# Causal mask of the softmax attention: added by VectorE in PSUM instead of by two TensorE products

## What is computed

```python
xn = x / jnp.maximum(l2, 1e-12) * scale_norm * gamma
qkv = jnp.einsum('bnc,fc->bnf', xn, w_qkv)          # 16 sequences, n = 256, 8 heads of 128
q = q * scale_attn
sim = jnp.einsum('bihd,bjhd->bhij', q, k)           # 256 x 256 per sequence and head
sim = jnp.where(causal_mask, neg, sim)              # j > i is masked
attn = jax.nn.softmax(sim, axis=-1)
out = jnp.einsum('bhij,bjhd->bihd', attn, v)
return jnp.einsum('bnf,cf->bnc', out.reshape(b, n, DIM_INNER), w_out)
```

## Time and profile before

| | |
|---|---|
| median of 3 runs | 3316.56 us (3315.86 to 3318.93) |
| the profiled execution | 3332.27 us, of it the profiled span 3330.6 us |
| mean granted TensorE clock | 0.879 of full speed |
| attention stage, first to last row maximum (127 units apart) | 1030.7 to 1386.0 us |
| busy in the span | PE 2336.7 us (70%), DVE 2420.9 (73%), ACT 1562.2 (47%), POOL 1600.5 (48%) |

### The profile page before, as it was taken

How to read it: one execution, slowest core, us unless ns; L and a number is a source line. 1 busy time by engine, 2 the same in 40 slices (tenths; PEclk the granted TensorE clock), 3 DMA queues, 4 the chain that set the end, 5 groups by cost and what they waited for, 6 DMA issues and landing times. The chain is left out here.

```text
span 3330.6 us, 60036 instructions
## 1 busy us (share of the span) xinstructions
PE 2336.7 (70%) x16660; PEld 1743.5 (52%) x16660; DVE 2420.9 (73%) x5876; ACT 1562.2 (47%) x3151; POOL 1600.5 (48%) x1352
## 2 busy tenths in 40 slices
PE   6636666754928999758343777678888847788887
PEld 2212222233827888648232555466767624676766
DVE  3479999963546666534446777489999966999998
ACT  2355455521714555326222444356666623566665
POOL 0176666614030000040324444289999901999996
PEclk9869899985968999959676999789999965999999
DMA  1000000012010000111100000100000000000000
GB/s 45 0 0 0 0 0 0 0 51 84 24 44 20 0 0 0 52 32 41 41 13 1 2 0 0 29 1 0 0 0 0 0 3 0 1 0 0 0 0 26
DMA packets 61385, 42.72 MB, mean 13 GB/s; under 512 B 7795, under 2 KB 55940, under 8 KB 61190
## 3 DMA queue, kind: packets, MB, share of 16 engines
q1 hardware_dynamic: 56070, 32.09, 3.4%
q0 software_dynamic: 4096, 8.40, 0.8%
q10 hardware_dynamic: 1120, 1.06, 0.1%
HBM read 27.38 MB, written 14.16 MB: 12 GB/s over the span
## 5 line engine op out<-in xcount | busy, mean ns | idle before, releaser
L1601 POOL TENSOR_TENSOR k7a_psums<-k7a_sims 128x1024 f32<-128x1024 f32 x224 | 422.8, 1912 | 189.4 <-ACT k7a_sims L1707 159.0
L1601 POOL TENSOR_TENSOR k5a_psums<-k5a_sims 128x1024 f32<-128x1024 f32 x224 | 422.7, 1913 | 77.3 <-ACT k5a_sims L1707 48.1
L725 POOL TENSOR_TENSOR mc_hc<-mc_h,mc_cs 128x512 f32<-128x512 f32 x256 | 324.8, 1269 | 149.7 <-DVE mc_h L708 149.1
L1661 PE MATMUL k7a_pw<-g_ident,k7a_w 128*128 128x128 f32 x2048 | 272.7, 279 | 87.7 <-DVE k7a_hid L1793 47.9
L1661 PE MATMUL k5a_pw<-g_ident,k5a_w 128*128 128x128 f32 x2048 | 272.2, 279 | 84.8 <-DVE k5a_hid L1793 47.9
L708 DVE TENSOR_TENSOR_SCAN mc_h<-mc_dA,mc_dbu 128x512 f32<-128x512 f32 x256 | 310.0, 1211 | 0.0
L1661 PEld LDWEIGHTS k7a_pw<-g_ident,k7a_w 128*128 128x128 f32 x2048 | 223.5, 141 | 147.9 <-DVE k7a_w L1784 92.2
L1661 PEld LDWEIGHTS k5a_pw<-g_ident,k5a_w 128*128 128x128 f32 x2048 | 223.2, 141 | 145.2 <-DVE k5a_w L1784 89.6
L637 PE MATMUL mc_y<-mc_hc,g_ident 128*128 128x512 f32 x512 | 257.7, 626 | 45.0 <-DVE m_sz L694 43.0
L667 ACT ACTIVATE mc_dA<-m_delta,m_A 128x510 f32 (+1 forms) x256 | 176.6, 690 | 227.3 <-DVE mc_h L708 227.2
L1784 DVE SCALAR_TENSOR_TENSOR k5a_w<-k5a_psums,k5a_best,k5a_lift 128x1024 f32<-128x1024 f32 x224 | 279.0, 1269 | 0.5 <-ACT k5a_lift L1722 0.3
(11 more groups left out here) (589 smaller groups left out, 5936.7 us busy)
## 6 DMA issues: line engine op xcount, KB each, us to landing
e_ZS<-sorted_rows SPq DMA_DIRECT2D x8, 640.0 KB, 7.4
sorted_out<-e_YS SPq DMA_DIRECT2D x8, 640.0 KB, 3.6
e1p_w<-in_L_ffn_W_dram SPq DMA_DIRECT2D x16, 256.0 KB, 5.5
e3p_w<-in_L_ffn_W_dram SPq DMA_DIRECT2D x16, 256.0 KB, 5.4
sorted_rows<-e_ZS SPq DMA_DIRECT2D x1, 2560.0 KB, 10.9
g_X<-in_L_attn_a_x_dram SPq DMA_DIRECT2D x8, 256.0 KB, 6.0
out_dram<-g_X SPq DMA_DIRECT2D x1, 2048.0 KB, 8.7
sorted_rows<-e_YS,e_slot POOLq DMA_INDIRECT x64
```

What stands on the lines that cost most here:

```text
L725: nc.gpsimd.tensor_tensor(hc[:, q % RH, :], h_[:, q % RB, :], cs[:, s % 2, :], ALU.mult).then_inc(outs, 1)
L1601: nc.gpsimd.tensor_tensor(psums[:, h - 1, :, :], rows_of(p, h), s2, ALU.add).then_inc(pooled, 1)
L1661: ins = nc.tensor.matmul(pw[:, j, :], w[:, h % WR, j * P:(j + 1) * P], env.ident[:, :], start=(h == 0 and j % 4 == 0), stop=(h == HD - 1 a ...
```

## The change

VectorE adds the mask. TensorE no longer computes the two bf16 products, and its two score products now start their blocks themselves. In `maxima`, a `tensor_tensor` adds `env.causal` (bf16, the same table for both blocks) to columns 0 to 127 and 256 to 383 of the score bank, read from and written to PSUM. Its own new semaphore `masked` is waited for by the first reduction.

```diff
@@ score (TensorE)
-                    nc.tensor.matmul(S[:, 0:P], env.identb[:, :], env.causal[:, :], start=True, stop=False)
-                    nc.tensor.matmul(S[:, 0:P], qT[:, u % 2, 0:P], ZT[:, bass.ds(base, P)], start=False, stop=True)
-                    nc.tensor.matmul(S[:, 2 * P:3 * P], env.identb[:, :], env.causal[:, :], start=True, stop=True)
-                    nc.tensor.matmul(S[:, P:3 * P], qT[:, u % 2, P:2 * P], ZT[:, bass.ds(base, SEQ)], start=False,
-                                     stop=True, skip_group_check=True).then_inc(scored, 1)
+                    nc.tensor.matmul(S[:, 0:P], qT[:, u % 2, 0:P], ZT[:, bass.ds(base, P)], start=True, stop=True)
+                    nc.tensor.matmul(S[:, P:3 * P], qT[:, u % 2, P:2 * P], ZT[:, bass.ds(base, SEQ)], start=True,
+                                     stop=True).then_inc(scored, 1)
@@ maxima (VectorE)
                     need(dve, scored, m + 1)
+                    diagonal = S[:, 0:3 * P].rearrange("p (k c) -> p k c", c=P)[:, 0:3:2, :]
+                    mask = env.causal[:, :].rearrange("p (o c) -> p o c", o=1).broadcast_to([P, 2, P])
+                    nc.vector.tensor_tensor(diagonal, diagonal, mask, ALU.add).then_inc(masked, 1)
                     need(dve, expd, m + 1 - R)
+                    need(dve, masked, m + 1)
                     nc.vector.tensor_reduce(nm[:, u % R, 0:1], S[:, 0:P], AX, ALU.max, negate=True)
```

More of the change, by code:

```diff
@@ L1318, in attention @@
             py, pout = ps("py", [P, 512]), ps("pout", [P, 512])
-            valued, asked, q_in, scored, maxed, expd, inverted, scaled, turned, t_in, mixed, y_in, made, added = (
-                sem(x) for x in ("valued", "asked", "qin", "scored", "maxed", "expd", "inverted", "scaled", "turned",
+            valued, asked, q_in, scored, masked, maxed, expd, inverted, scaled, turned, t_in, mixed, y_in, made, added = (
+                sem(x) for x in ("valued", "asked", "qin", "scored", "masked", "maxed", "expd", "inverted", "scaled", "turned",
                                  "tin", "mixed", "yin", "made", "added"))
```

## The result

| | before | after |
|---|---|---|
| median | 3316.56 us (3315.86 to 3319.19, 5 runs) | 3335.18 us (3332.50 to 3337.26, 5 runs) |
| profiled execution, its span | 3332.27, 3330.6 | 3333.46, 3331.7 |
| first to last row maximum of the stage | 355.3 us | 373.1 us |

What follows compares the result with a forecast made beforehand. TensorE bounds the steady units, VectorE the residual one. Groups of eight go from 22.66 to 23.18 us; 15 x 0.52 + 7 x 0.03 = 8, plus 1 for imperfect catching up, on 3316.6 gives 3326 us, range 3314 to 3336.

Steps and rivals of the forecast that it cites:

- rival 3: The wait behind VectorE's addition is dear, 0.52 to 0.60 us, VectorE deciding from about 0.55: 3331 to 3338 us, chance 0.15.
- The likeliest case: Whole-kernel forecast with the addition at 0.42 to 0.52 us: 3323 to 3331 us, chance 0.45.
- an addition above 0.5: Sign in the profile after that the forecast is wrong: addition over 0.5 us, pointing to a dear wait behind it.
- 0.45 us from its start to the start of the reduction: VectorE's mask addition: 0.41 us long, plus 0.04 until the first reduction starts.
- 0.06 to the next `mix` but one: Hand-off from the end of ScalarE's `y_copy` to TensorE's `mix`, read behind another copy: 0.06 us.
- a pair of units: Two units set by the loop through TensorE, VectorE and ScalarE: 4.63 us, including 0.10 for a `mix` that waited.
- the unit with `project`: Unit containing `project`: 5.86 us before, less TensorE's 0.23 of mask products, 5.63 after.
- `rows`: Extra VectorE time in the unit with `rows`: 0.63 us, making that unit 2.76.
- the loop of a pair in the kernel before: Three-engine loop over two units with mask products: 4.31 us, below TensorE's 4.58, so it never showed.
- 1, that TensorE stays the bound: VectorE's slack takes up the additions: down to 3287 us, a partial gain to 3305 the most imagined; chance 0.08.
- 2, a cheap addition: Addition at 0.33 to 0.42 us from start to start, loss and gain cancel: 3316 to 3323 us, chance 0.30.
- 4, the clock: TensorE's gaps lower its clock; a tenth of its time at half clock gives some 15 us, 3341; chance 0.02.

## Why the prediction was right in kind and short by half

**Right.** Slower, in this stage alone, at full clock. TensorE gets gaps at `mix`, released by `y_copy` three times in a group (49 times, 17.4 / 49 = 0.36 each) and by VectorE's copy in the unit with the residual (1.18 at 1228.29 in the timeline). VectorE waits 3.4 to 3.5 at `project`. All of this stood in the list of what would show it, though the groups measured 23.7 to 24.1 and not 23.2 to 23.4. The median, 3335.18, lies in the range, 0.8 us below its upper edge, and that is in part luck: the range reaches to 3336 only to hold most of rival 3. The likeliest case, 3323 to 3331, is missed: 18.6 us were lost, not 9. And one of the prediction's own signs of being wrong came, "an addition above 0.5", if it is taken from start to start as rival 3 takes it: 0.53.

**The steps that were mis-sized**, as the prediction put them:

| step | said | measured |
|---|---|---|
| "0.45 us from its start to the start of the reduction" | 0.45 | 0.53 |
| "0.06 to the next `mix` but one" | 0.06 | 0.15 |
| a pair of units | 4.63 | 4.81 |
| the unit with the residual | 3.40 | 3.47 |
| the unit with `project` | 5.63 | 5.76 |
| `rows` | 0.63 | 0.51 |
| the one behind the residual and that with `rows` | 4.89 | 4.90 |
| the loop of a pair in the kernel before | 4.31 | 4.42, at the loop's head 4.63 |
| group of eight behind the loop's head | 23.18 | 23.74 |
| group at the loop's head, over before | 0.52 | 1.14 |

1. *The addition.* Its length was right to 0.02. The 0.04 behind it was read from L1484 to L1486, an instruction with one wait; the reduction has two. Moving one away brought 0.46 and 4.1 us. That is shown. By the prediction's own 0.8 us for each 0.01, an addition of 0.53 would have put it at 3332, so this is the larger part of the miss.
2. *`y_copy` to `mix`.* I took the 0.06 from VectorE's copy that let `mix` go. Behind ScalarE's copy it is 0.14 to 0.15, in this kernel, in the one without a mask and in the one with the copies exchanged. Up to the `ask` behind `mix` it is 0.15 + 0.73 = 0.88 where I had 0.06 + 0.65 + 0.10 = 0.81.
3. *A held `mix`.* I charged 0.10 per pair, for the unit that visibly waits. In fact the other unit is held as well, by 0.04, and it takes 0.73 too. This accounts for `project`: 5.86 - 0.23 + 0.04 + 0.08 = 5.75, against 5.76.
4. *The unit with `rows`.* Its 4.89, with the one behind the residual, came out at 4.90 by luck. The 0.63 was read in the kernel before from a reduction that was still waiting for its score: in its trace TensorE's `score` ends where `turn` starts, at 1229.41, and 0.20 for the hand-off gives 1229.61, against 1229.62. What `rows` costs VectorE is 0.51, and the 0.12 too much hid most of what the two additions there cost more.
5. *The loop's head.* I took the same 0.52 for both kinds of group; they lost 1.14 and 1.06. At the head a pair measures 2.19 + 2.75 = 4.94, the 0.13 over 4.81 lying between the reduction and the exponential. Before, the loop of 4.42 with the same 0.13 and the 0.08 of a held `mix` makes 4.63, as measured, and TensorE's own 4.58 covered all but 0.05 of it. What delays the exponential there was not tried.

Of the group's 0.56 over the forecast, 0.36 lie in the two pairs, 0.13 in `project` and 0.07 in the residual unit. Times 15 the 0.56 is 8.4 us; the head's 0.08 in every second group is 0.6. With the 8 of the forecast that makes 17.0, against 17.8 in the traces; the rest lies in the units at the two ends of the stage, which the forecast had not walked.

With the one loop of 4.81 the experiments come out, with only the 0.07 of the wait and 0.02 of `y_copy`'s 0.27 taken from kernels of their own: 4.29 without the addition (4.27 by sum), 4.73 with one wait (4.74), 4.54 with the copies exchanged (4.54), 4.46 with both (4.47), 5.03 with the products kept (5.04). What I had treated as a lesser limit, some hundredths under TensorE, is the bound of half the units in each of these five.

**The rivals.** 1, that TensorE stays the bound: fell; even without any addition it isn't (stage 340.2, not 326). 2, a cheap addition: fell: the addition costs 0.53 from start to start, and it costs 0.53 with SBUF as its destination too. 3, a dear wait behind the addition, 0.52 to 0.60 and 3331 to 3338: both its distance and its time came. But its reason, that VectorE alone decides, is not it, since exchanging ScalarE's copies would then have changed nothing. The prediction had the sum for it wrong, too: "it decides from about 0.55 on" doesn't follow from its own terms, by which two units of VectorE, 3.36 and two additions, pass the loop's 4.18 and one addition only when the addition costs 0.82. I had argued against it that the reduction has no address arithmetic ahead; that it has a second wait I didn't count. 4, the clock: it stayed at 1.00 with TensorE busy 21.58 of 23.74.

**The rule on PSUM** (the Trainium skill, "Perfetto Trace Analysis", "Optimizing Scalar/DVE Operations": some 65 ns more for a VectorE access to PSUM) would have ended 5 us higher and nearer the result. The runs don't bear it out for the write: 433 against 424 ns for the same addition into PSUM and into SBUF, and 0.53 to the reduction in both. It would have come nearer for a reason that isn't there.

## What to carry to other kernels

Before moving work off the busiest engine, go round every loop between engines, each hand-off taken from the same pair of engines, and compare its sum with the bound: here 4.42 against 4.58 left 0.16 us of room in two units (none at the loop's head), and the change put 0.54 into the loop where it took 0.23 out. Work put on an engine with a busy share of 66% is paid in full where that engine stands in such a loop; try first to make the work cheaper where it is. And put waits that were met long ago ahead of the instruction before, not between a producer and its consumer on one engine.

## What the hardware showed that I had not expected

- **A second wait that is already met costs time**: the reduction starts 0.10 us behind the addition's end with two waits, 0.04 with one (0.53 and 0.46 from start to start, in the kernel after and with the wait moved).
- **A product that is held is also slower**: fp32 `mix` takes 0.73 when ScalarE's copy holds it, 0.65 when nothing does, and in between when it is held by less than 0.08: its second part starts 0.44 behind the copy's end. In the kernel after the weight load starts 0.03 ahead of a held product, in the kernel before 0.11 ahead of a free one. Holding the product and not the load was not tried.
- **Hand-offs differ by pair of engines**: 0.15 us from ScalarE's copy to TensorE's `mix`, 0.06 from VectorE's (1227.67 + 0.56 to 1228.29).
- **An fp32 product behind a short bf16 product is slower**: the 128 fp32 columns take 0.27 behind a mask product of 128 columns, 0.23 behind one of 256, 0.22 with none (1236.98 to 1237.20). The 256 columns take 0.49 behind a mask product, 0.43 and 0.44 without. So two mask products cost 0.22 a unit, and one that does the same work 0.11.
